# A fused DLRM tower on one core: the last pair layer by seven products with the batch as result rows, the added fields ranked, one load further up

## The reference

```python
e = stack([tbl_f[ids[:, f]] for f in range(8)], axis=1)      # (512, 8, 1024)
x_not = take(e, not_idx, axis=1)                             # fields 2, 3
t = tanh(relu(x_not @ Wn1 + bn1) @ Wn2 + bn2)
iv = e.at[:, not_idx, :].set(t)
def pair_fuse(pairs, W1, b1, W2, b2):
    v = concatenate([take(iv, pairs[:, 0], 1), take(iv, pairs[:, 1], 1)], -1)
    return relu(v @ W1 + b1) @ W2 + b2
and_out = pair_fuse(and_pairs, Wa1, ba1, Wa2, ba2)           # pairs (0,1), (2,3)
or_out  = pair_fuse(or_pairs,  Wo1, bo1, Wo2, bo2)           # pair  (4,5)
z = (and_out.sum(1) + or_out.sum(1) + einsum('bfh,f->bh', iv, remaining)) / count
h = maximum(concatenate([z, dense_ctx], 1) @ W_top1 + b_top1, 0)
y = maximum(h @ W_top2 + b_top2, 0) @ W_top3
```

## Time and profile before

| | us |
|---|---|
| median of 3 runs | 544.79 |
| runs | 541.98 to 545.34 |
| profiled execution | 548.29 |
| its span, first to last instruction | 546.3 |
| PE busy in the span | 530.2 |
| DVE busy | 356.7 |
| ACT busy | 248.6 |
| POOL busy | 234.7 |

### The profile page before, as it was taken

The page is one execution under the profiler, slowest core; times in us unless marked ns, Lnnn a source line. Parts: engine busy times, 40 slices in busy tenths (PEclk is TensorE's granted clock), DMA queues, the critical chain, the costliest instruction groups (busy, mean ns, idle before and its releaser), DMA issues.

```text
span 546.3 us, 6174 instructions
## 1 busy us (share of the span) xinstructions
PE 530.2 (97%) x2392; PEld 440.5 (81%) x2392; DVE 356.7 (65%) x370; ACT 248.6 (45%) x301; POOL 234.7 (43%) x176
## 2 busy tenths in 40 slices
PE   5999989987999999999999999999999999999998
PEld 5988878765888888888888888888888888888885
DVE  6487997968876775888547678742332874245832
ACT  3584666515456644442537444323243432142343
POOL 5548887898117653140087017655445300000000
PEclk9999999997999999999999999999999999999999
DMA  8966956456965675366199425999999972331000
GB/s 268 324 136 146 218 150 209 136 122 146 193 124 170 144 138 167 78 108 123 39 205 319 123 93 176 276 247 247 247 247 247 246 254 79 116 92 40 0 1 0
DMA packets 38607, 87.31 MB, mean 160 GB/s; under 512 B 4305, under 2 KB 4561, under 8 KB 38578
## 3 DMA queue, kind: packets, MB, share of 16 engines
q0 software_dynamic: 18624, 49.29, 41.5%
q1 hardware_dynamic: 19522, 37.51, 21.5%
q10 hardware_dynamic: 432, 0.11, 0.1%
HBM read 86.90 MB, written 0.00 MB: 159 GB/s over the span
## 4 chain that ended last, share of the span: by engine, by line
PE 79%; POOL 13%; issue 3%; DMA 2%; ACT 2%; DVE 1%; ACTq 0%
PE PS L1070 76%; POOL XR L490 12%; POOL WR L512 1%; DMA WR<-weights 1%; DMA XR<-table,rows 1%; PE PS L1248 1%; PE PS L1099 1%; PE PS L1220 1%; ACT WO L598 1%; DMA XR<-ints 0%; PE PS L1255 0%; ACT XR L732 0%; ACT XR L657 0%; DVE WO L804 0%; POOL XR L479 0%
## 5 line engine op out<-in xcount | busy, mean ns | idle before, releaser
L1070 PE MATMUL PS<-XO,WO 128*128 128x512 f32 (+1 forms) x2256 | 508.1, 387 | 8.2 <-DVE WO L804 8.2
L1070 PEld LDWEIGHTS PS<-XO,WO 128*128 128x128 f32 x2256 | 419.7, 189 | 94.3 <-DVE WO L804 9.7
L598 ACT ACTIVATE WO<-WR 128x1024 fp32r<-128x1024 f32 x93 | 98.6, 1060 | 242.0 <-PE PS L1070 226.1
L804 DVE TENSOR_TENSOR WO<-WR,WO 128x1024 fp32r<-128x1024 f32 x93 | 113.9, 1224 | 144.7 <-ACT WO L598 144.5
L490 POOL DMA_INDIRECT XR<-table,rows x96 | 130.3, 1357 | 61.1 <-issue 28.3
L628 ACT ACTIVATE XO<-XR 128x1024 fp32r<-128x1024 f32 (+1 forms) x76 | 79.3, 1045 | 3.2 <-DVE XR L949 3.2
L512 POOL DMA_DIRECT2D WR<-weights x30 | 37.5, 1627 | 86.7 <-DVE WO L804 39.8
L880 DVE TENSOR_TENSOR XO<-XR,XO 128x1024 fp32r<-128x1024 f32 x60 | 73.1, 1220 | 1.0 <-ACT XO L628 0.9
L575 POOL DMA_INDIRECT XR<-table,rows_rest x32 | 52.4, 1638 | 40.2 <-DMA XR<-table,rows_rest 38.0
L897 DVE STREAM_TRANSPOSE XR<-XR 128x1024 f32<-128x1024 f32 x26 | 55.8, 2153 | 3.1 <-DMA XR<-table,rows 3.1
L949 DVE TENSOR_TENSOR XR<-XR 128x1024 f32<-128x1024 f32 (+1 forms) x32 | 38.5, 1216 | 0.0
(11 more groups left out here) (72 smaller groups left out, 113.4 us busy)
## 6 DMA issues: line engine op xcount, KB each, us to landing
WR<-weights SPq DMA_DIRECT2D x71, 512.0 KB, 4.8
WR<-weights POOLq DMA_DIRECT2D x30, 512.0 KB, 7.0
XR<-table,rows POOLq DMA_INDIRECT x110, 4.2
XR<-table,rows_rest POOLq DMA_INDIRECT x32, 12.7
XR<-dense_t SPq DMA_DIRECT2D x3, 32.0 KB, 2.9
XR<-w_dense SPq DMA_DIRECT2D x3, 32.0 KB, 3.1
XR<-ints SPq DMA_DIRECT2D x1, 84.0 KB, 2.1
XR<-identity ACTq DMA_DIRECT2D x1, 64.0 KB, 3.5
```

The source lines that it names most:

```text
L598: nc.scalar.activation(WO[:, n % 2, 0, :], WR[:, slot, :], ACT.Copy).then_inc(w_hi, 1)
L804: V_.tensor_tensor(WO[:, n % 2, 1, :], WR[:, raw_slot(n), :], WO[:, n % 2, 0, :].bitcast(FP32), ALU.subtract).then_inc(w_lo, 1)
L1070: mm = nc.tensor.matmul(PS[:, bank, cols], WO_t[:, slot, ws, i, k, :], XO[:, x0 + k, xs, cols], start=first and k == 0 and n == 0, stop=la ...
```

## The change

1. `Z` becomes seven products too, over quadrants of 512 by 256: 14 entries (7 products by the two matrices Wa2 and Wo2, which add up in PSUM). A quarter of these entries is 6 matmuls. The operands change places: x is stationary (128 of the batch by 128 of H), weights are moving (4 blocks of 128 columns, 256 apart), so that a result has the batch on its partitions, as rows. A piece of Wa2 or Wo2 is now 4 blocks of 256 columns in place of 2 of 512.
2. 8 sums of operands (`Z_SUMS`), 16 combinations of result rows (`Z_ROWS`) and 6 copies out of PSUM are added; 16 transfers that add weights are added on POOL behind the 32 gathers. The remaining fields' tiles are added to rows by DVE (`z_combine`, step 0, reading every eighth element), and the finished rows of z are turned by 32 transposes: 16 ahead of the last entry of Z, 16 behind the first quarter of TOP.
3. `setup_rest_rows` (t = 88) ranks the remaining fields: gather 0 takes the first of them, gather 1 the second, and so on; gathers past their number get an index above `bounds_check`, and move nothing.
4. Slots: raw pieces have 15 (8 of them in free parts of XR), split weights of Z have 4. In OZ four raw slots go round in place of seven. W_top2 is loaded ahead of the dense inputs.

```diff
-Z_PARTS = [(6, 0, 0), (6, 1, 0), (7, 0, 0), (7, 1, 0), (7, 1, 1), (7, 0, 1), (6, 1, 1), (6, 0, 1)]
+Z_ORDER = (P1, P2, Q5, Q6, Q3, Q7, P4)
+Z_BANK = {P1: 4, Q6: 4, Q7: 4, Q5: 0, Q3: 0, P2: 6, P4: 6}
+Z_KEPT = {P1: "C11", Q5: "C22", Q6: "C12"}
...
+Z_RAW = {j: (4, 5, 6, 7) for j in (P1, Q5, Q6, P4)}
+Z_RAW.update({P2: (0, 8, 9, 10), Q3: (1, 2, 3, 0), Q7: (11, 12, 13, 14)})
...
+SPLIT_W_AT = {n: 2 * n - 4 if Z_PIECE + 1 < n < TOP_PIECE + 1 else 2 * n - 2 for n in range(2, PIECES)}
...
+SETUP_AT, REGS_AT, REST_ROWS_AT = 44, 50, 88
+Z_SUMS = sorted([(122, S1, 0), (126, S3, 0), (130, S2, 0), (150, S1, 1), (154, S3, 1), (158, S2, 1), (162, S4, 0),
+                 (166, S4, 1)])
...
-                             (59, 51), (55, 52), (60, 53), (61, 54), (62, 55)):
+                             (59, 51), (55, 52), (72, 53), (73, 54), (74, 55)):
                 load_after(n, split)
-            for n in range(63, PIECES - 1):
-                load_after(n, n - 7)
+            for n in range(60, 71):
+                load_after(n, n - 4)
+            load_after(71, 67)
             sp.wait_ge(x_lo, x_done(Z - 1, 1))
+            for n in range(92, 96):
+                load(n)
+            for n, split in ((76, 68), (88, 69), (89, 70), (90, 71)):
+                load_after(n, split)
+            sp.wait_ge(zr_ready, 2 * KT)
+            for n in (75, 77, 78, 79):
+                load(n)
+            for n, split in ((91, 76), (100, 77), (101, 78), (102, 79), (103, 88)):
+                load_after(n, split)
...
-            pool.wait_ge(setup_done, 1)
+            pool.wait_ge(rest_rows, 1)
...
                         bass.IndirectOffsetOnAxis(ap=rows_rest[:, b, f:f + 1], axis=0),
+                        bounds_check=zero_row - 1 if f else zero_row, oob_is_err=False,
                         compute_op=ALU.add if f else ALU.bypass,
...
+            def add_z(j, half, h):
+                n = Z_PIECE + 2 * (z_entry(j, half) - Z) + h
+                if j == Q7:
+                    pool.wait_ge(raw_in[raw_slot(n)], RAW_LOADED[n])
+                else:
+                    split = Z_PIECE + 2 * (z_entry({Q5: P1, Q6: Q5, P4: Q6}[j], half) - Z) + h
+                    pool.wait_ge(w_lo, split + 1)
+                pool.dma_start(raw_part(n), z_rows_of(n, ADDED), accum_op=ALU.add).then_inc(w_sum[raw_slot(n)], 16)
...
+            for j in (Q7, Q5, Q6, P4):
+                for part in parts:
+                    add_z(j, *part)
...
+                    for bt in range(2):
+                        if h == 0 and half == 0:
+                            z_bank_free(j, bt)
+                        for k in range(2):
+                            for i, (ws, xs) in enumerate(((0, 0), (1, 0), (0, 1))):
+                                mm = nc.tensor.matmul(PS[:, Z_BANK[j] + bt, :],
+                                                      XO[:, x0 + 2 * h + k, xs, P * bt:P * (bt + 1)],
+                                                      w_columns(n, ws, k),
...
+            entry(TOP, True, False, lambda m: pe.wait_ge(z_out, m + 1), None, 1,
+                  lambda: turn_z(0, Z_ROW_COUNT["C21", 1, 1]))
+            entry(TOP + 1, False, False, no_wait, dense_part, 1)
```

More of the change, by code:

```diff
@@ L90 @@
 PIECES = QUARTERS // 2 + 1
+Z_PIECE, TOP_PIECE = FIRST[Z] // 2, FIRST[TOP] // 2
 DENSE_K = 8 * KT + TOP1_PIECES
@@ L159, in x_done @@
 def x_done(e, kk):
-    return x0_done(1, 2 * e + kk) if e < 2 else 8 + 2 * (e - 2 - sum(e >= i for i in KEPT_X)) + kk + 1
+    if e < 2:
+        return x0_done(1, 2 * e + kk)
+    if e < Z:
+        return 8 + 2 * (e - 2) + kk + 1
+    if e < TOP:
+        return 8 + 2 * (Z - 2) + e - Z + 1
+    return 8 + 2 * (Z - 2) + TOP - Z + 2 * (e - TOP) + kk + 1
 def x0_done(h, pair):
@@ L286, in dlrm_tower @@
         cnt = keep(1)
+        row_z = keep(BT * F)
+        nth = keep(F * F)
         def rest_tile(b):
@@ L722, in _ @@
                             nc.scalar.activation(to, dense_raw[:, B * i:B * (i + 1)], ACT.Copy).then_inc(dense_hi, 1)
-                    if t and t % 2 == 0:
-                        split_w(t // 2 + 1)
+                    for n in range(2, PIECES):
+                        if SPLIT_W_AT[n] == t:
+                            split_w(n)
                     for kk in range(2):
@@ L1003, in pair_sum, with z_to_top @@
+            def z_to_top(i, k):
+                dve.wait_ge(z_turned, i + 1)
+                V_.scalar_tensor_tensor(out=XR[:, Z_BUF, k, :], in0=PS[:, (k + 4) % 8, :], scalar=inv[:, 0:1],
+                                        in1=XR[:, 0, k, :], op0=ALU.mult, op1=ALU.add).then_inc(z_out, 1)
             def pair_sum(t):
@@ new lines, in turn_z @@
+            def turn_z(first, rows):
+                pe.wait_ge(z_rows, rows)
+                upper, lower = ("C12", "C22") if first else ("C11", "C21")
+                for k in range(first, first + 4):
+                    for b in range(BT):
+                        row = z_row(upper if b < 2 else lower, b % 2)
+                        turn = nc.tensor.transpose(PS[:, (k + 4) % 8, P * b:P * (b + 1)],
+                                                   row[:, P * (k % 4):P * (k % 4 + 1)], ident[:, :].bitcast(FP32))
+                    turn.then_inc(z_turned, 1)
```

339 lines of the change are left out of this document (236 added, 103 removed).

## The result

| | before | changed |
|---|---|---|
| median of 14 runs each, same chip, us | 544.73 | 539.38 |
| lowest to highest | 541.98 to 547.88 | 532.93 to 541.63 |
| profiled execution, us | 548.29 | 538.54 |
| its span, us | 546.3 | 536.7 |

The medians differ by 5.4 us. The ratio is 0.989, with a 95% interval of 0.9858 to 0.9922: 6.0 us faster, 4.2 to 7.7 (it is taken of the means, without one run of the changed kernel that fell in a slower state of the chip). The median, 539.38, is 3.9 us above the predicted 535.5.

The account below looks back on a forecast made before the run. PE was taken to bound the kernel, so matmuls removed are time removed: -10.9 for matmuls, +0.6 at the border, +1.0 for late adds, -9.3 us in all, from 544.8 to 535.5 us; range 532 to 550.

Parts of the forecast that it names:

- the border: Z to TOP: 16 transposes wait for DVE's last row combination, a new PE stall of 0.6 us.
- late adds: Z, Q6's weight splits: PE stalls while adding transfers wait in POOL's queue; 0.2 us by the sum, 1.0 taken for bursts.
- the term of the matmuls: PE in Z: 336 matmuls in place of 384, 48 fewer at 0.2267 us each, 10.9 us saved.
- A: Rival, chance 0.15: adds in Z moderately dearer, 4.2 us each, giving 9.8 us of stall and 544.3 us.
- C: Rival, chance 0.07: ranking doesn't work in time, gathers past the bound take as long, adds come late; 547.5 us.
- Four blocks as moving operand: PE in Z: moving operand of four non-adjoining 128-column blocks costs 0 extra, with 19 us as the far end.
- Rival D: Chance 0.06: new shapes cost PE 19 us (554.5 us), or push DVE above 77.9 us in Z.
- DVE in Z: Quarters 144 to 199: DVE needs 70.6 us against PE's 77.9, fits at 91%; strided combinations taken at 0.6 us each.
- D: In the DMA sum for Z: the engines' time for one 512 KB add, taken as 3.4 us.
- B: Rival, chance 0.12: the adding queue becomes the bound at Q6's splits, 5.6 us per add, 26.6 us of stall, 561 us.
- my inequality: DMA in Z, quarters 132 to 174: no stall if 17 loads, 12 adds and 5 us fit in 71.1; sum 71.3.
- The end of the gathers: POOL ahead of Z's adds: eight real gathers end near 356 us, 24 empty ones near 392; cost 0.

Follow-up runs that it names:

- the last: Changed kernel with Q7's adds ahead of gather pass 7 alone, memset on POOL, TOP's second weight split one quarter later: 529.90 us, stretch from Z through TOP 102.3.
- The border to TOP: Changed kernel with Q7's adds ahead of the last two gather passes, plus memset on POOL and TOP's second weight split one quarter later: 536.71 us, ratio 0.9894 to before.

## Why the prediction was nearly right

Predicted for the stretch: -10.9 for matmuls, +0.6 at the border, +1.0 for late adds, -9.3. Measured: -10.9, +1.8, +3.5, -5.5. The direction and the term of the matmuls were right. That 539.38 lies within 532 to 550 is luck in part: the range went up to 550 for rivals A and C. A fell, and C is only near to what took the 3.8 us: the gathers ended between my 392 and its 431, but what came late first were plain loads, not the adds that it named.

- **The matmuls** were right to 0.1 us, once nothing stood in their way. The price per matmul was DVE's old rhythm, and the spacing after is the same 227 ns. The Trainium skill ("TensorE: Matmul & The Clock Gate", Back-to-back issue gap) would have made it 6.3 us, an estimate from its 131 ns; the rows of Z and TOP show 227.
- **Four blocks as moving operand**, taken at 0 with 19 us as the end: 0. Rival D fell by this half.
- **DVE in Z**, taken at 70.6 of 77.9 us. The stride was the wrong choice: 1.17 us per combination where I took 0.6, even above the 1.07 kept as the end. Without the stride TOP's first start is 1.0 us earlier and Q6's late start 0.9 us less late, where I had let the stride count only at the border; that last part is in the 3.5 us of the adds too, since it is gone without either. DVE still fitted: in the kernel with two passes it was busy 69.3 of the 78.0 us of Z, so D's other half fell as well. The rule of the Trainium skill ("SBUF — State Buffer", the note on cachelines under Door 1), that reads which pass to a new 16-byte line each time pay a penalty, speaks for the dearer price, and the run with contiguous reads agrees: 684 ns in place of 1169.
- **The border**, 0.6 predicted, 1.8 measured (104.1 in the run with no adds less 102.3 in the last). The wait that I had, that of the last transposes, came out right: 0.8 by the starts, and its two combinations took 0.68 each. The one that I lacked is TOP's very first product (0.8 us idle, 1.0 by the starts). It waited for DVE's split of x, and DVE came there late because two strided combinations and the memset stood further ahead, of which my order of the border said nothing. Contiguous reads removed this wait, and so did the edits of "The border to TOP":

```profile
495.33 1.18 DVE L1200 TENSOR_TENSOR XR<-PS,XR 128x512 f32<-128x512 f32 x1
...
502.61 0.68 DVE L1191 TENSOR_TENSOR XR<-XR,PS 128x512 f32<-128x512 f32 x1
...
504.34 0.68 DVE L1191 TENSOR_TENSOR XR<-XR,PS 128x512 f32<-128x512 f32 x1
```

- **The adds**, the term that was mis-sized. D was too dear in my sum: adds in 1 KB pieces, alone from 447 to 458 us, moved:

```profile
DMA packets 2163, 2.17 MB, mean 197 GB/s; under 512 B 64, under 2 KB 2158, under 8 KB 2162
...
q0 software_dynamic: 2157, 2.14, 122.8%
```

 That is 2.7 us per 512 KB where I took 3.4, and no less than the 187 GB/s of 2 KB pieces: by bytes, not by packets. Rivals A and B fell by it (A from 4.2, B from 4.25). With D = 2.7 my inequality gives no stall at all, yet 3.5 us were lost. So the inequality was the wrong test: it asked for Q6's last piece over the whole window, while the first start to be late was P2's second, fed by plain loads (pieces 78 and 79, for which ACT waited 2.90 and 1.87 us). The next, Q5's, came late because DVE was behind; only the third, Q6's, had waited for an add (3.60 us). ACT's waits from 405 to 512 us, of which 5.9 us of the first row are for loads and 2.3 for adds:

```profile
ACT XO L734 <- DMA XR<-weights: 8.2, 5, 2.9
...
ACT WO L734 <- DMA WR<-weights: 4.2, 2, 3.6
```

- **The end of the gathers**, the step that failed. I put it near 392 us: eight gathers out by 356, then 24 times POOL's 1.25 to 1.6 us. The eight were out by 351, but the 24 took from 353.56 to 407.4: 42.4 us of instructions (1.77 in the mean, some above 2 us, why stays open), 6.2 us for the 0.30 between two, which my sum lacked, and 5.2 us of waits for the last real rows to land. POOL then gave out eight adds from 407 to 428 us, and since their packets go in turn with the loads', they took about half the packets from 1 KB loads just when P2 and its successors needed them; from 400 to 410 us the DMA had moved only 121 GB/s. I had called this "0". Two passes in all bring back the whole 3.5 us, and so does issuing Q7's adds one pass sooner (102.3 with the border eased; with the border's 1.8 that would be 104.1, an estimate).
- **Rival C**, that the ranking would do nothing in time, had 13 us as its price. The ranking did its work, and without it the loss was 37 us and the kernel 6% slower than before, so I had under-priced this outcome by a factor of three. For that price the rule of packets in turn was missing, though the earlier trace rows showed it.
- **The rank computation** and W_top2's load, at 0: as predicted. PE has no idle time from 140 us to the start of Z.
- **The signs**: 227 ns and 48 matmuls fewer came true. The adds landed in 6.5 to 18.7 us, where I had 6 to 12, and the gathers ended at 407, where I had 395.

## What to carry to other kernels

Before sharing DMA between two queues, compare their packet sizes, not only their bytes: with both queues full, cutting one side's pieces in half cuts its share. When a change frees time on PE, sum the path of every piece that is due early in the stage, not only of the last one, and place work that does nothing (empty passes here) behind the transfers that somebody waits for, but not behind a queue that it must itself wait for.

## What the runs showed of the hardware

- Two full DMA queues (POOL's and SP's) were served packet for packet: 1142 to 1142 with packets of 3.6 and 1.6 KB in the mean, 1097 to 1098 at 3.7 and 1.9, 1808 to 1801 at 1 KB each. The Trainium skill ("DMA: Bandwidth & Descriptors", Issuing engines are not separate DMA queues) has that they interleave, which the rows bear out; the one-for-one is read from these rows.
- An adding transfer moves 197 GB/s in 1 KB and 187 in 2 KB pieces, against 343 on average for loads, nearly all in 1 KB pieces, from 392 to 400 us of the changed kernel.
- A gather whose indices all lie past the bound moves no rows (551 packets of POOL's queue with 0.00 MB from 389 to 400 us), but still costs POOL at least 1.86 us. Its landing waits behind what stands in its queue: 7.31 us behind four adds, none when it was issued ahead of them.
- DVE takes 1.17 us for a sum of 512 elements per partition when it reads one operand at every eighth element, and 0.68 us for the same sum when both are contiguous.
- In the 38 us without a matmul the granted clock fell to 0.50 of full, the lower of its two levels (1.2 of 2.4 GHz), and the first 12 matmuls behind took 5.19 us in place of 2.88. After 5.07 us idle, with Q7's adds behind Q5's, it was 0.50 as well. The row of the long stall:

```profile
440.00:450.00 10.00, 0.00 (x0) 0.00 (x0) 0.00 (x0) 0.00 (x0) 5.17 (x4) 0.50 1.17 251
```

 The row is of the kernel without the bound; its columns are window, us, busy us of PE, PEld, DVE, ACT, POOL, granted clock, DMA share and GB/s.
